# The negated row maxima of an attention stage: turned by DVE in 32 by 32 squares and sent from ACT's queue, in place of a TensorE transpose and SP's queue

## What is computed

```python
x = x + 0.5 * ffn(layernorm(x))      # hidden 2048, weights replaced by their signs, relu
x = x + attention(layernorm(x))      # 16 heads of 32, 2 batches: 32 heads in all
x = x + 0.5 * ffn(layernorm(x))
# attention of one head, q, k, v of shape 2048 x 32:
scores = q @ k.T * SCALE             # 2048 x 2048
probs = softmax(scores)              # over the keys
out = probs @ v
```

## Time and profile before

| what | us |
|---|---|
| median of three runs | 2858.61 (2857.84 to 2862.39) |
| the profiled execution, its own time | 2858.64 |
| its span, first to last instruction | 2856.6 |
| PE busy | 2840.1 (99%) |
| DVE busy | 2063.3 (72%) |
| ACT busy | 1607.4 (56%) |
| POOL busy | 1367.3 (48%) |
| mean granted TensorE clock | 0.999 of full speed |

### The profile page before, as it was taken

How to read it: one execution, slowest core, us unless ns; L and a number is a source line. 1 busy time by engine, 2 the same in 40 slices (tenths; PEclk the granted TensorE clock), 3 DMA queues, 4 the chain that set the end, 5 groups by cost and what they waited for, 6 DMA issues and landing times.

```text
span 2856.6 us, 38045 instructions
## 1 busy us (share of the span) xinstructions
PE 2840.1 (99%) x14316; PEld 1947.7 (68%) x14316; DVE 2063.3 (72%) x3084; ACT 1607.4 (56%) x2851; POOL 1367.3 (48%) x486
## 2 busy tenths in 40 slices
PE   9999999999999999999999999999999999999999
PEld 7888888787755555555555555555555568888887
DVE  5655556778888888888888888888888456665553
ACT  6444434333277777676767777676767654333333
POOL 0000000000088998999999989998989720000000
PEclk9999999999999999999999999999999999999999
DMA  5111102555489998999999999999999972222200
GB/s 192 32 57 30 30 30 67 199 193 190 150 180 191 198 216 188 203 204 200 209 196 197 211 193 198 208 199 209 199 194 200 219 204 60 59 60 59 74 15 30
DMA packets 134982, 424.27 MB, mean 149 GB/s; under 512 B 23824, under 2 KB 41488, under 8 KB 98832
## 3 DMA queue, kind: packets, MB, share of 16 engines
q0 software_dynamic: 31824, 231.75, 39.5%
q1 hardware_dynamic: 102976, 190.11, 23.1%
HBM read 121.91 MB, written 67.63 MB: 66 GB/s over the span
## 4 chain that ended last, share of the span: by engine, by line
PE 94%; DVE 3%; DMA 1%; ACT 1%; issue 1%; POOL 0%; SPq 0%; DVEq 0%; ACTq 0%; POOLq 0%
PE bank L1130 18%; PE bank L1126 17%; PE bank L1160 16%; PE bank L655 15%; PE bank L634 15%; PE bank L796 7%; PE bank L497 3%; PE bank L1187 1%; DMA x<-xT 1%; PE bank L276 0%; DVE qkv_o_lo L760 0%; DVE norm_cent L122 0%; ACT att_p L1110 0%; DVE x_out L595 0%; DMA qkv_raw<-upT 0%
## 5 line engine op out<-in xcount | busy, mean ns | idle before, releaser
L1041 DVE TENSOR_REDUCE att_row_max<-bank 128x1 f32<-128x512 f32 x2048 | 1248.3, 679 | 207.6 <-PE bank L1130 207.6
L990 POOL TENSOR_TENSOR att_acc<-att_acc,att_p 128x2048 f32<-128x2048 f32 x216 | 1073.8, 4971 | 16.1 <-ACT att_p L1110 8.8
L1110 ACT ACTIVATE att_p<-bank 128x512 f32<-128x512 f32 x1792 | 919.4, 619 | 285.0 <-PE bank L1126 281.6
L1130 PE MATMUL bank<-att_k,att_q 96*128 96x512 f32 x2048 | 833.0, 409 | 1.4 <-DVE att_row_max L1041 0.7
L1126 PE MATMUL bank<-att_q,att_k 98*128 98x512 f32 x2048 | 809.2, 398 | 2.5 <-ACT att_p L1110 2.5
L1130 PEld LDWEIGHTS bank<-att_k,att_q 96*128 96x128 f32 x2048 | 387.3, 189 | 272.5 <-DVE att_row_max L1041 121.2
L617 ACT ACTIVATE ffn_hid<-bank,up_s 128x512 f32<-128x512 f32 x256 | 176.2, 688 | 510.1 <-PE bank L655 495.5
L1126 PEld LDWEIGHTS bank<-att_q,att_k 98*128 98x128 f32 x2048 | 385.9, 189 | 113.2 <-ACT att_p L1110 14.8
L1160 PE MATMUL bank<-att_p,att_v 128*32 128x512 f32 x3584 | 433.3, 600 | 0.0
L568 DVE TENSOR_TENSOR ffn_hid_lo<-ffn_hid,ffn_hid_hi 128x512 fp32r<-128x512 f32 x256 | 174.7, 690 | 345.3 <-ACT ffn_hid_hi L620 344.6
L655 PE MATMUL bank<-hi,ffn_up_w 128*128 128x512 f32 x1024 | 399.9, 391 | 3.0 <-DVE lo L221 3.0
(11 more groups left out here) (123 smaller groups left out, 2398.2 us busy)
## 6 DMA issues: line engine op xcount, KB each, us to landing
att_dma_acc<-att_p POOLq DMA_DIRECT2D x161, 1024.0 KB, 10.3
att_dma_acc<-att_dma_acc POOLq DMA_DIRECT2D x30, 1024.0 KB, 11.9
att_dma_acc<-att_acc POOLq DMA_DIRECT2D x30, 1024.0 KB, 6.9
att_q<-q_hi SPq DMA_DIRECT2D x64, 256.0 KB, 4.0
att_k<-k_hi SPq DMA_DIRECT2D x64, 256.0 KB, 6.5
x<-x_after_ffn SPq DMA_DIRECT2D x14, 1024.0 KB, 7.1
x_after_ffn<-x_out SPq DMA_DIRECT2D x8, 1024.0 KB, 9.6
q_hi<-qkv_o_hi SPq DMA_DIRECT2D x32, 256.0 KB, 2.3
```

What stands on the lines that cost most here:

```text
L990: self.nc.gpsimd.tensor_tensor(self.acc[H % 2][:], a[:], self.tile(H, kt)[:], ALU.add).then_inc(self.summed, 1)
L1041: self.nc.vector.tensor_reduce(self.row_max[odd][:, qt, q:q + 1], m[:], axis=AX.X, op=ALU.max).then_inc(self.m_read, 1)
L1110: self.nc.scalar.activation(into[:, q * CH:(q + 1) * CH], self.score_bank(H, kt, q)[:], ACT.Exp, scale=SCALE).then_inc(self.exp_done, 1)
L1130: self.nc.tensor.matmul(m[:], self.q_st[T % NB][0:KQ, qt * P:(qt + 1) * P], self.k_st[T % NB][0:KQ, q * CH:(q + 1) * CH], start=True, stop ...
```

## The change

- PE's transpose is gone, with its slot in the round of banks (65 slots a head) and the waits that belong to it.
- DVE writes the negated maxima into the first 16 columns of a 128 x 32 tile (the other 16 are set to zero once), turns the tile with one instruction in squares of 32 by 32, and makes the high and the low part from SBUF, 128 x 32 each. These come right after `negate`, with waits of DVE on its own semaphore between them.
- In the turned tile, partition 32 i + t holds queries 32 i to 32 i + 31 of tile t. A row of 2048 is therefore put together from four DMAs, one per i, each with 16 pieces of 32 numbers (128 bytes). High and low part make eight DMAs per head in place of two.
- For heads 1 to 31 these eight are issued from ACT's instruction stream, before exponential 48 of the head before (`ROWS_AT` = 45 + 3), after that key tile's two waits. For head 0 they are issued from SP's list, where the two were.
- With the slots gone the sums bank falls otherwise: in the last head PE waits once more for the copy of the sums before last.

```diff
-SUMS_AFTER = TURN_AFTER = 4
-SUMS_AT = TURN_AT = GROUP_ENDS[SUMS_AFTER]
-SLOTS = UNITS + 2
+SUMS_AFTER = 4
+SUMS_AT = GROUP_ENDS[SUMS_AFTER]
+ROWS_AT = SUMS_AT + 3
+SLOTS = UNITS + 1
...
-NEG = 3
+NEG = 4
+TURN = 32
+NEG_LOADS = 2 * 16 * (P // TURN)
...
-    def max_rows(self, sp, H):
+    def max_rows(self, eng, H):
         for r, rows in enumerate((self.neg_hi, self.neg_lo)):
-            sp.wait_ge(self.neg_dve, NEG * H + 2 + r)
-            sp.dma_start(f32(self.q_st[H % NB][KQ + r:KQ + r + 1, :].rearrange("o (t p) -> o t p", p=P)),
-                         f32(rows[:])).then_inc(self.neg_loaded, 16)
+            eng.wait_ge(self.neg_dve, NEG * H + 3 + r)
+            row = self.q_st[H % NB][KQ + r:KQ + r + 1, :].rearrange("o (t i p) -> o i t p", i=P // TURN, p=TURN)
+            for i in range(P // TURN):
+                eng.dma_start(f32(row[:, i, :, :]), f32(rows[i * TURN:i * TURN + KT, :])).then_inc(self.neg_loaded, 16)
...
         if H > 0:
-            dve.wait_ge(self.neg_pe, H)
-        self.nc.vector.tensor_reduce(self.neg_max[:], self.row_max[H % 2][:], axis=AX.X, op=ALU.max, negate=True).then_inc(self.neg_dve, 1)
-
-    def rows_out(self, dve, H, t_ps):
-        dve.wait_ge(self.neg_pe, H + 1)
+            dve.wait_ge(self.neg_dve, NEG * H)
+        else:
+            self.nc.vector.memset(self.neg_max[:], 0.0).then_inc(self.neg_set, 1)
+            dve.wait_ge(self.neg_set, 1)
+        self.nc.vector.tensor_reduce(self.neg_max[:, 0:KT], self.row_max[H % 2][:], axis=AX.X, op=ALU.max, negate=True).then_inc(self.neg_dve, 1)
+
+    def rows_out(self, dve, H):
+
+        dve.wait_ge(self.neg_dve, NEG * H + 1)
+        self.nc.vector.transpose(self.neg_t[:], self.neg_max[:]).then_inc(self.neg_dve, 1)
+        dve.wait_ge(self.neg_dve, NEG * H + 2)
         if H > 0:
-            dve.wait_ge(self.neg_loaded, 32 * H)
-        self.nc.vector.tensor_copy(self.neg_hi[:], t_ps[0:KT, 0:P]).then_inc(self.neg_dve, 1)
-        dve.wait_ge(self.neg_dve, NEG * H + 2)
-        self.nc.vector.tensor_tensor(self.neg_lo[:], t_ps[0:KT, 0:P], f32(self.neg_hi[:]), ALU.subtract).then_inc(self.neg_dve, 1)
+            dve.wait_ge(self.neg_loaded, NEG_LOADS * H)
+        self.nc.vector.tensor_copy(self.neg_hi[:], self.neg_t[:]).then_inc(self.neg_dve, 1)
+        dve.wait_ge(self.neg_dve, NEG * H + 3)
+        self.nc.vector.tensor_tensor(self.neg_lo[:], self.neg_t[:], f32(self.neg_hi[:]), ALU.subtract).then_inc(self.neg_dve, 1)
...
             if kt == KT - LEAD and q == 0 and H + 1 < NH:
                 self.negate(dve, H + 1)
-            if p == TURN_AT - 1 and H + 1 < NH:
-                self.rows_out(dve, H + 1, self.turn_bank(H))
+                self.rows_out(dve, H + 1)
...
+            if QC * kt + q == ROWS_AT and H + 1 < NH:
+                self.max_rows(act, H + 1)
             act.wait_ge(self.s_ready, UNITS * H + QC * kt + q + 1)
...
-    def transpose_max(self, pe, H, t_ps):
-        pe.wait_ge(self.neg_dve, NEG * H + 1)
-        self.nc.tensor.transpose(t_ps[0:KT, 0:P], self.neg_max[:], self.ident[:]).then_inc(self.neg_pe, 1)
...
-        if u == TURN_AFTER and H + 1 < NH:
-            self.bank_free(pe, H, TURN_SLOT)
-            self.transpose_max(pe, H + 1, self.turn_bank(H))
         if u == sums_after(H) and H > 0:
             self.bank_free(pe, H, SUMS_SLOT)
+            if H == NH - 1:
+                pe.wait_ge(self.head_out.sums_copied, H - 1)
             self.sums(pe, H - 1)
...
-                    else:
-                        att.max_rows(sp, H + 1)
```

More of the change, by code:

```diff
@@ L846, in slot @@
 def slot(p):
-    return p + (p >= SUMS_AT) + (p >= TURN_AT)
-TURN_SLOT, SUMS_SLOT = TURN_AT, SUMS_AT + 1
+    return p + (p >= SUMS_AT)
+SUMS_SLOT = SUMS_AT
 AT_SLOT = {slot(p): p for p in range(UNITS)}
@@ L916, in __init__ @@
         self.row_max = [c.sb(f"att_row_max{i}", HEAD_AT + 4 + 0.25 * i, [P, KT, QC]) for i in range(2)]
-        self.neg_max = c.sb("att_neg_max", HEAD_AT + 4.5, [P, KT])
-        self.neg_hi, self.neg_lo = c.sb("att_neg_hi", HEAD_AT + 5, [KT, P], F32R), c.sb("att_neg_lo", HEAD_AT + 5.5, [KT, P], F32R)
+        self.neg_max, self.neg_t = c.sb("att_neg_max", HEAD_AT + 4.5, [P, TURN]), c.sb("att_neg_t", HEAD_AT + 4.625, [P, TURN])
+        self.neg_hi, self.neg_lo = c.sb("att_neg_hi", HEAD_AT + 5, [P, TURN], F32R), c.sb("att_neg_lo", HEAD_AT + 5.5, [P, TURN], F32R)
         self.m_ps, self.s_ps, self.o_ps = c.bank[0:4], c.bank[4:7], c.bank[7]
@@ L923, in __init__ @@
         self.m_ready, self.m_read = c.sem("att_m_ready"), c.sem("att_m_read")
-        self.neg_dve, self.neg_pe, self.neg_loaded = c.sem("att_neg_dve"), c.sem("att_neg_pe"), c.sem("att_neg_loaded")
+        self.neg_set, self.neg_dve, self.neg_loaded = c.sem("att_neg_set"), c.sem("att_neg_dve"), c.sem("att_neg_loaded")
         self.s_ready, self.exp_done, self.p_used = c.sem("att_s_ready"), c.sem("att_exp_done"), c.sem("att_p_used")
@@ L937, in sums_bank @@
         return self.m_ps[3] if H >= NH - 2 else self.m_ps[m_bank(H + 1, SUMS_SLOT)]
-    def turn_bank(self, H):
-        return self.m_ps[m_bank(H, TURN_SLOT)]
     def load(self, sp, X, pieces=range(6)):
@@ L1142, in first_maxima @@
             pe.wait_ge(self.m_read, n - 1)
-        if n == UNITS:
-            pe.wait_ge(self.neg_dve, NEG)
         self.maxima(self.first_bank(n), T, n % UNITS // QC, n % QC)
-    def transpose_max(self, pe, H, t_ps):
-        pe.wait_ge(self.neg_dve, NEG * H + 1)
-        self.nc.tensor.transpose(t_ps[0:KT, 0:P], self.neg_max[:], self.ident[:]).then_inc(self.neg_pe, 1)
     def out_tile(self, pe, H, kt):
@@ L1196, in bank_free @@
             pe.wait_ge(self.head_out.sums_copied, H)
-        elif old == TURN_SLOT:
-            pe.wait_ge(self.neg_dve, NEG * (H + 2))
         elif old < 0:
@@ L1206, in tensor_group @@
         if u == 0:
-            pe.wait_ge(self.neg_loaded, 32 * (H + 1))
+            pe.wait_ge(self.neg_loaded, NEG_LOADS * (H + 1))
             pe.wait_ge(self.ones_set, min(H + 1, NB))
@@ L1475, in _ @@
                             att.negate(dve, 0)
-                        if (n, t) == FIRST_TURN:
-                            att.rows_out(dve, 0, att.m_ps[2])
+                            att.rows_out(dve, 0)
                 for H in range(NH):
@@ L1592, in _ @@
                             att.first_maxima(pe, first + b)
-                        if (n, t) == FIRST_TURN:
-                            att.transpose_max(pe, 0, att.m_ps[2])
                 pe.wait_ge(qkv.qk_read, 8 * NCH)
@@ L1606, in beside @@
                                 pe.wait_ge(att.m_read, UNITS * NH)
-                                pe.wait_ge(att.neg_dve, NEG * NH)
                                 pe.wait_ge(wo_done, DT + 1)
```

## The result

| | before | after |
|---|---|---|
| median, us | 2858.99 (2857.84 to 2862.39) | 3178.42 (3176.1 to 3181.11) |
| ratio to before | | 1.1116 (interval 1.1102 to 1.1129) |
| span of the profiled execution | 2856.6 | 3175.9 |
| mean granted TensorE clock | 0.999 | 0.95 |

The change makes the kernel 319 us slower, by 11%. The forecast, 2852, was wrong, and so was the range, 2848 to 2990. In the prediction the numbers of some groups of rows are shifted. Its rows 6 are group 11 above, 7 is 14, 8 is 6, 9 is 7, 11 is 8, 12 is 9, 13 is 12 and 14 is 13. From here on groups are named by their own numbers.

A forecast was written before the change was run, and what follows sets the result against it. PE was taken to bound the kernel, busy 2840.1 of 2856.6 us. The profiled 2858.64 less 6.7 for the transposes, all else hidden, gave 2851.9, stated as 2852; the forecast's own range was 2849 to 2855, the overall range 2848 to 2990.

The forecast's parts named there:

- PE: On PE, the bounding engine: removing 32 transposes of 0.21 us each saves 6.7 us.
- DVE: On DVE: turn, copy and subtraction at 0.28 us each, 0.04 between dependent ones; costs nothing.
- the cover: On DVE: 1.8 us of idle time before its next work hides the turn, copy and subtraction.
- SP: On SP's queue: two issues a head go, 0.52 and 1.38 us; PE doesn't wait, so nothing is gained.
- ACT, the start: On ACT's queue: issues start once the high part is written, 1334.70, ahead of pending exponentials; other end 1337.97, with exponential 47.
- ACT, the price: On ACT's queue: 0.46 us an issue, eight in 3.7 us, just hidden before exponential 48; upper end 10.1 us.
- the prediction's rival by which SP's move blocks ACT's: SP's move of the sums (1.31 us) blocks ACT's issue in between: 0.95 us a head, 2881; no chance of its own.
- The sum: Whole kernel: 2858.64 less 6.7 is 2851.9, given as 2852, all else hidden; chance 0.44.
- A: Rival, ACT ahead of exponential 48: issues in a row cost the low part's 1.37 us, 10.1 in all; 3040; chance 0.22.
- B: Rival, ACT's queue: issues start late, with exponential 47, 2.9 us a head; 2942; chance 0.20.
- Landing: Row transfers: the last issue lands 6.8 (at most 8.0) us later, by 1346.4, leaving 2.7 us before the next head.
- C: Rival, start of the next head: 128-byte pieces land late, PE waits 5.3 us a head; 3017; chance 0.04.

The follow-up runs named there:

- experiment 8: Experiment 1 with both parts made by reductions before one shared turn, and four issues of 32 pieces from SP: 2851.62 us, ratio 0.9976 to the kernel before.
- experiment 7: The changed kernel, eight issues still on ACT, with DVE's copy and subtraction made by reductions: 3177.31 us, ratio 1.1110 to the kernel before.
- experiment 1: The changed kernel with its eight issues sent from SP instead of ACT: 2940.28 us, ratio 1.0286 to the kernel before.
- experiment 6: Experiment 1 with DVE's copy and subtraction made by reductions over one or two elements: 2875.64 us, ratio 1.0058 to the kernel before.
- experiment 2: The kernel before, transpose kept on PE, with its two moves issued from ACT ahead of exponential 48: 2897.59 us, ratio 1.0134.
- experiment 3: The changed kernel with the eight ACT issues one exponential earlier, ahead of exponential 47; run once: 3144.0 us.
- experiment 4: The changed kernel with the eight ACT issues spread, one ahead of each of exponentials 46 to 53; run once: 3006.04 us.
- experiment 5: The kernel before, transpose kept on PE, with each row sent from SP in four pieces, eight issues a head: 2895.11 us, ratio 1.0122.
- experiment 9: Experiment 8 with its four issues sent from ACT ahead of exponential 48 instead of SP: 3025.35 us, ratio 1.0574 to the kernel before.

## Why the prediction was wrong

**PE: right.** There is no transpose, and the sums stand right behind the output pieces. The 6.7 us are real and stand alone in experiment 8.

**DVE: the cost was right where nothing holds it, the cover was not.** The turn takes 0.21 us where I took 0.28, and in 21 of 32 heads all is ready in time. In 11 heads an instruction of 0.19 us was held for 4.3 to 5.4 us, which is far past the 1.8 us of idle time that was to hide it. The old copies read the bank and took 0.28 in each head; the new ones read and write SBUF, and that was the difference to ask about. It was no measurable part of the loss (experiment 7), but is worth 65 us as soon as ACT is free (experiments 1 and 6). The Trainium skill ("SBUF — State Buffer", SBUF: two separate sides) has a rule for this: a DVE instruction in a two-port mode or with two SBUF inputs and a GpSimd instruction take one pair of ports by an exclusive lock, and the loser is blocked whole. The trace agrees in what is held (a copy and a two-input subtraction, never a reduction or the turn) and in the release at 1455.35 and 1455.41. In its records DVE's instruction starts 0.30 us before POOL's, so who took the pair first is not shown.

**SP: right, at nothing.** Its two issues bounded nothing.

**ACT, the start: this step failed.** "I take it that ACT's issues also start while older exponentials are still to be done" rested on one row of POOL. That row shows an issue that starts while the addition ahead of it runs, not one that passes an instruction which has yet to start. ACT does the same: the issue starts with the exponential ahead (experiments 2, 3 and 4). The high part was there at 1450.15 and the first issue began at 1453.33. The Trainium skill ("Perfetto Trace Analysis", Sequencer Loop) has the sequencer push a compute instruction into a queue and go on; here it was never more than one exponential ahead. By the prediction's clock the start is 1337.97, its other end.

**ACT, the price: this step failed too.** "I take 0.46" came from stores of another shape. The row of the same shape in the same stretch, 1.37 for the low part, was the right one. The 0.52 of the high part is a first issue and no mean: experiment 2 shows the same pair, 0.52 and 1.37. The same rows had the pattern: the third move in that queue, the sums', took 1.31 as well. Measured are 9.0 us for eight on average, 9.6 as the median, against 3.7 in the prediction. Another queue (1, 5) and twice the pieces (8) leave a median of 1.2 to 1.3, and experiment 4 didn't part the issues. An issue alone takes 0.5 under full load, one in a row under light load 0.6; right behind another and under POOL's load it is mostly 1.3. Nor does it come from both queues issuing at once (the prediction's rival by which SP's move blocks ACT's): in 30 of 32 heads after, SP's second move of the sums (L421) overlaps an issue of ACT, and it takes 0.33 to 0.35 there, against 0.34 before.

**The sum: the rivals weren't added.** A had the price with the early start, 3040, and B the late start with the low price, 2942. Each was given its own chance, and the case that both hold was given none, although either can hold without the other and both had a row for them. With both it is 1337.97 + 10.1 - 1338.75 = 9.3 us, times 31 is 289, less 6.7: 3141. That is beyond the range's end of 2990.

**The clock: missing.** No step asked what a stall does to PE's clock. It adds 1.8 us in the head shown, and 1.8 x 31 = 56 makes 3197. The nine heads with cheaper issues (about 7.2 us in place of 10.1) take back 26, and the typical 9.7 of the others 8: 3163, against 3178 measured. The 15 us between were not traced; the sum is an account made afterwards, so its closeness proves little, and the tests are experiments 1, 2 and 9.

**Landing: right for ACT.** The issue ends at 1463.39 and the slowest landing is 7.8 us later, 1471.2; the waits show no wait for rows worth the name. C came true only where the issues are on SP, and by the time that eight of them take, not by their landing.

Two things stay open. Why an issue right behind another mostly costs 1.3 us while the DMA engines are taken, and sometimes 0.6, was not settled. The shape is not all of it, since the loads of keys, in a row too, took 0.42 before and had medians of 1.15 and 1.23 in the kernel after. Neither is the DMA share: head 0's first two issues took 0.63 and 0.59 at a share of 1.03, without POOL's traffic. And nothing was taken away by itself: neither issues truly apart nor a kernel without POOL's accumulating moves was tried, and the load's part rests on head 0 and on experiment 3.

## What to carry to other kernels

Price a DMA issue by the row of the same shape, under the same load and at the same place in a row of issues, count issues and not bytes, and on a compute engine's queue start them with the last compute instruction ahead, never earlier. Where two unknown costs add on one engine, give the case that both are at their bad end its own time and chance, and add what TensorE's clock takes after a stall of some microseconds. A smaller version of the idea did pay: both parts made before one turn, four issues, and those on the idle queue.

## What the hardware showed that was not expected

- An issue of a small move from SBUF to SBUF that starts alone on its queue costs 0.5 us (0.65 with 32 pieces) even when the DMA engines are fully taken. Right behind another it costs 0.59 us at a mean DMA share of 0.29 (head 0), 0.63 at 0.39 and mostly about 1.33 at 1.02, whether it has 16 or 32 pieces, on ACT's or on SP's queue.
- A DVE instruction of 0.19 us beside POOL's addition was held for 5.2 us. A `tensor_reduce` over one element does the same copy in 0.17 to 0.22 and was never held.
- Behind a stall of PE of 3.7 us (experiment 9) the granted clock was 0.50 for the next 6.7 us. In the head shown of the kernel after it was 0.50 through the stall of 6.3 us and for the 2.4 us behind it. In experiment 2, with 1.2 us a head, the mean stayed at 0.999.
